# Graph attention on one core: the last half of the mask loaded, signed and packed as two quarters, and the last pair's first row decoded and gathered by itself

## The chip, the cores and the metric

The kernel runs on one core of one Trainium2 chip. The metric is the device time of one execution in microseconds (us). The kernel before takes 815.76 us, the median of three runs from 815.68 to 815.86.

## The reference

The input `x` has 8192 rows of 128 floats, `adj` is a mask of 8192 x 8192 int32 whose entries are 1 with a probability of 0.000488281, so that a row has about four neighbours, and `attn` holds two vectors of 128. The layer is graph attention on a normalised `x`, with `x` added at the end:

```python
h = jnp.maximum(_layernorm(x, axis=-1), 0.0)
s_i = h @ attn[:d]
s_j = h @ attn[d:]
e = jax.nn.leaky_relu(s_i + s_j.T, negative_slope=0.2)
e = e + jnp.where(adj > 0, jnp.float32(0.0), neg_inf)      # neg_inf = -1e9
alpha = jax.nn.softmax(e, axis=1)
x = x + alpha @ h
```

Nearly all of the input is the mask: 268 MB. A row without a neighbour has a softmax over all 8192 nodes, so it needs every row of `h`.

## The kernel before

**Tiles, halves, pairs.** The 8192 rows are cut into 64 tiles of 128 rows, one row to a partition, and two tiles make a pair (32 pairs, `PAIRS`; p = 0 to 31). The row of a pair's first tile is called the first row below, that of the second tile the second row. The mask of a tile comes in two halves of 4096 columns (`HALF`, 2 MB), so there are 128 halves. SP's queue loads them (`load_pair`, `L414`) into a ring of five (`adj_ring`); the load of half n waits until half n - 5 has been signed.

**From the mask to candidates.** ACT signs each half (`sign_tile`, `L614`): one instruction turns the int32 into small floats in `sign_ring` (four halves) and accumulates the row's count into `degree`. TensorE packs the signs of the columns into 1024 words a row, in PSUM (`pack_tile`): two matmuls place a constant (`L1358`), then four matmuls a half add the digits (`L1367`). When a half is signed, its four matmuls are let go, by the semaphore `signed`. DVE takes the eight largest of every quarter of the words (`max_tile`, four MAX8 at `L770`), which gives 32 candidates a row (`cand`).

**From candidates to neighbours.** `find_pair` (`L777` to `L825`) decodes the candidates of both rows together: it unpacks each word into eight codes (`L787`, an AND with a mask of bits, into `terms`), takes the largest eight codes of each row (MAX8 at `L794`, `L795`), joins the two lists and turns the codes into row numbers, `near_id`. A pair has 12 slots (`SLOTS`): four of the first row (`OWN`), four that serve both rows, four of the second. POOL gathers slot by slot 128 rows of `h` from a table in DRAM, one indirect DMA a slot (`gather_pair`, `L521`), into a ring of three pairs (`near`). `flag_pair` (`L834` to `L856`) compares what was found with `degree` and flags the rows with more neighbours than that.

**From neighbours to the output.** `score_pair` (`L907` to `L923`, DVE) adds up the scores of the 16 edges of a pair, `exp_pair` (`L631`, ACT) exponentiates them, `weigh_pair` (`L966` to `L970`, DVE) makes weights of them. For most pairs DVE adds up the weighted rows too, two turns later. The last three pairs (29, 30, 31; `BODY` is 29) are mixed on TensorE: ACT writes each of the 16 weight columns as a diagonal matrix (`write_diagonals`, `L644`), TensorE multiplies the gathered rows by them (`mix_pair`, `L1403` and `L1407`; the profile counts two matmuls for each product in float32), and ACT copies the sums out (`close_pair`, `L649`).

**Other rows.** Flagged rows are listed by a matmul with a one-hot matrix (`key_pair` on DVE, `L862` and `L866`; `L1393` on TensorE) and worked on 128 at a time, with 16 gathers for each such list (`find_deep`, `L979` to `L1012`, and `L532` on POOL). Rows without a neighbour, called lone, are collected for the pairs from 25 on by `lone_mark` (`L1064` to `L1074`), `lone_compact` (`L1083` to `L1106`), `lone_spreads` on TensorE (`L1424`, `L1427`), `lone_bounds` (`L1113` to `L1129`) and `lone_part` (up to `L1147`), exponentiated by ACT (`L670`) and summed over all 8192 rows by 64 steps of TensorE (`lone_matmuls`, `L1443`). A loop for rows that fit nowhere (the far loop) stands at the end and runs one step here.

**Order.** Each engine works through its own stream in the order in which the code lists it, and semaphores tie the streams together; nothing reorders them. The order is written out by hand. In the last turn, p = 31, DVE's stream reads: `max_tile(62)`, `key_pair(30)`, `score_pair(29)`, `max_tile(63)`, `find_pair(31)`, `flag_pair(31)`, `lone_mark`, `key_pair(31)`, `weigh_pair(29)`, `lone_compact`, `score_pair(30)`, `find_deep`, `weigh_pair(30)`, `mark_severe`, `lone_bounds`, `size_loop`, `lone_part`, `score_pair(31)`, `weigh_pair(31)`, the far loop. ACT's stream after the last signing: the diagonals of pair 29, `exp_pair(30)`, `close_pair(29)`, diagonals of pair 30, closing and storing it, the exponentials of the lone rows, then the same for pair 31. TensorE has the products of pair 29 ahead of `lone_spreads`, and those of pairs 30 and 31 behind it.

## Time and profile before

| What | Value |
| --- | --- |
| Median of the timed runs | 815.76 us (815.68 to 815.86) |
| Profiled execution | 813.88 us, of which the span that the profile shows is 812.1 us |
| PE (TensorE matmul) | busy 368.9 us, 45% of the span |
| DVE (VectorE) | busy 615.4 us, 76% |
| ACT (ScalarE) | busy 534.3 us, 66% |
| POOL (GpSimd) | busy 504.5 us, 62% |
| Chain that ended last | DMA 74%, issue 14%, POOL 5%, ACT 3%, DVE 3%, PE 1% |

The profile is of one execution, whose 813.88 us is 1.88 us below the median of the timed runs. Busy shares are means over the whole span. The profile also shows the span in 40 equal slices of 20.3 us: the DMA engines are at 0.9 or more from the 2nd to the 36th slice and move some 390 to 430 GB/s, and in the last four slices it is 132, 33, 56 and 8 GB/s. In these four DVE is at 0.8, 0.9, 0.3 and 0.3, TensorE at 0.6, 0.6, 0.4 and 0.7, POOL at 0.5, 0.5, 0.7 and 0.3. The chain is read from the last instruction back to what released each step; "issue" is time in which the profile shows nothing that the engine waited for.

### The profile page before, as it was taken

Reading aid. Unit: us, or ns where it says so; the run is one execution under the profiler, and the core shown is the slowest. Engines: PE = TensorE matmul, PEld = TensorE weight load, DVE = VectorE, ACT = ScalarE, POOL = GpSimd, SP = SyncE. Lnnn points to the kernel's source line nnn. Section 1 sums busy time; section 2 is a strip of 40 time slices with the busy share of each in tenths; the row PEclk is TensorE's granted clock in tenths of the full one; section 3 lists DMA queues with packets and bytes.
Section 4 is the critical chain, followed back from the end, with each engine's and each line's share of the span. In section 5 each row is a group of like instructions: output and inputs, shape, how many; then the busy total and the mean of one; then the engine's idle time right before and its main releaser. Section 6 shows DMA issues by size and latency. Waiting matters only on the chain.

```text
span 812.1 us, 6394 instructions
## 1 busy us (share of the span) xinstructions
PE 368.9 (45%) x1359; PEld 168.9 (21%) x1378; DVE 615.4 (76%) x2028; ACT 534.3 (66%) x410; POOL 504.5 (62%) x526
## 2 busy tenths in 40 slices
PE   1455334444433344444444344443444545646647
PEld 1222011111111111111111011111111213424636
DVE  6898288677758667797769666797769799898933
ACT  4985676676676767676675767667666677767430
POOL 6720777755556767755547677556547667765573
PEclk9875565555555555555555565555555556877679
DMA  8999999999999999999999999999999999993120
GB/s 344 406 408 429 393 406 408 405 414 411 410 391 412 411 408 406 405 406 407 410 403 406 409 407 408 407 412 413 411 412 408 409 407 411 406 410 132 33 56 8
DMA packets 39719, 301.59 MB, mean 371 GB/s; under 512 B 10682, under 2 KB 17149, under 8 KB 22272
## 3 DMA queue, kind: packets, MB, share of 16 engines
q1 hardware_dynamic: 24032, 277.04, 83.9%
q0 software_dynamic: 15360, 23.88, 8.6%
q10 hardware_dynamic: 288, 0.26, 0.1%
q8 instruction: 11, 0.18, 0.1%
q14 instruction: 28, 0.23, 0.1%
HBM read 303.76 MB, written 8.98 MB: 385 GB/s over the span
## 4 chain that ended last, share of the span: by engine, by line
DMA 74%; issue 14%; POOL 5%; ACT 3%; DVE 3%; PE 1%; POOLq 0%; SPq 0%; DVEq 0%
DMA adj_ring<-in_adj_dram 73%; POOL near L521 3%; ACT sign_ring L614 2%; POOL near_m L532 2%; DMA x_all<-in_x_dram 1%; DVE one_hot L725 1%; ACT h_all L626 1%; PE words L1367 0%; DMA out_dram<-adj_ring 0%; POOL out_dram L562 0%; DVE sums L955 0%; DVE cand L770 0%; POOLq L597 0%; DVE terms L950 0%; POOL adj_ring L553 0%
## 5 line engine op out<-in xcount | busy, mean ns | idle before, releaser
L614 ACT ACTIVATE sign_ring<-adj_ring,half_neg 128x4096 fp8e3<-128x4096 int32 x128 | 474.9, 3710 | 215.3 <-DMA adj_ring<-in_adj_dram 215.3
L521 POOL DMA_INDIRECT near<-h_table,near_id x384 | 391.1, 1019 | 234.2 <-issue 122.8
L1367 PE MATMUL words<-sign_ring,pack_w 128*128 128x512 bf16 x511 | 220.2, 581 | 357.9 <-ACT sign_ring L614 357.6
L770 DVE MAX8 cand<-words 128x8 f32<-128x256 f32 x256 | 90.8, 416 | 113.3 <-PE words L1367 113.3
L1367 PEld LDWEIGHTS words<-sign_ring,pack_w 128*128 128x128 bf16 x512 | 53.9, 125 | 520.7 <-ACT sign_ring L614 453.1
L955 DVE TENSOR_REDUCE sums<-terms 128x128 f32<-128x1024 f32 x58 | 112.2, 1935 | 2.0
L532 POOL DMA_INDIRECT near_m<-h_table,id_m x64 | 65.1, 1017 | 19.5 <-issue 19.5
L950 DVE TENSOR_TENSOR terms<-near,weight 128x512 f32<-128x512 f32 (+1 forms) x87 | 73.4, 871 | 0.0
L1358 PE MATMUL words<-place,place_w 128*128 128x512 bf16 x110 | 55.2, 587 | 7.1 <-DVE key L862 3.7
L1393 PEld LDWEIGHTS listing<-cand,one_hot 128*128 128x128 f32 x128 | 33.0, 316 | 10.6 <-issue 7.3
L1348 PE MATMUL listing<-h_all 128*1 128x128 f32 x128 | 18.6, 316 | 24.8 <-ACT h_all L626 24.8
L1393 PE MATMUL listing<-cand,one_hot 128*128 128x34 f32 x128 | 27.6, 358 | 0.2 <-DVE one_hot L866 0.2
L614 ACT ACTIVATION_READ_ACCUMULATOR sign_ring<-adj_ring,half_neg 128x1 f32 x128 | 23.8, 186 | 0.0
L1443 PE MATMUL rank<-h_all,x_all 128*64 128x129 f32 x128 | 21.0, 343 | 4.6 <-DVE key L862 4.6
L787 DVE TENSOR_TENSOR terms<-cand_i,code_mask 128x512 int32<-128x512 int32 x32 | 22.1, 692 | 1.1
L958 DVE SCALAR_TENSOR_TENSOR x_all<-sums,inv,x_all 128x128 f32<-128x128 f32 x58 | 20.4, 351 | 2.1
L756 DVE TENSOR_TENSOR near<-h_all,terms 128x2048 f32<-128x2048 f32 x8 | 21.4, 2681 | 0.0
L644 ACT ACTIVATE adj_ring<-ident,adj_ring 128x128 f32<-128x128 f32 x48 | 14.3, 387 | 10.7 <-DVE adj_ring L970 10.7
L1443 PEld LDWEIGHTS rank<-h_all,x_all 128*64 128x64 f32 x128 | 20.3, 181 | 4.9 <-DVE key L862 4.9
L626 ACT ACTIVATE h_all<-x_all,terms 128x128 f32<-128x128 f32 x48 | 18.8, 480 | 2.3 <-DVE terms L742 2.3
L498 POOL TENSOR_SCALAR h_all<-x_all,terms 128x128 f32<-128x128 f32 x16 | 13.0, 828 | 11.7 <-DVE terms L742 11.7
L907 DVE TENSOR_SCALAR score<-near,h_all 128x8 f32<-128x8 f32 x32 | 7.0, 220 | 17.1 <-DMA near<-h_table,near_id 17.1
(271 smaller groups left out, 521.7 us busy)
## 6 DMA issues: line engine op xcount, KB each, us to landing
adj_ring<-in_adj_dram SPq DMA_DIRECT2D x128, 2048.0 KB, 24.6
near<-h_table,near_id POOLq DMA_INDIRECT x384, 6.4
h_table<-h_all POOLq DMA_DIRECT2D x4, 1056.0 KB, 14.8
x_all<-in_x_dram SPq DMA_DIRECT2D x4, 1024.0 KB, 9.7
out_dram<-x_all SPq DMA_DIRECT2D x30, 128.0 KB, 24.2
near_m<-h_table,id_m POOLq DMA_INDIRECT x64
out_dram<-x_all ACTq DMA_DIRECT2D x2, 128.0 KB, 3.1
adj_ring<-h_table SPq DMA_DIRECT2D x1, 132.0 KB, 2.6
```

Of the source, the lines that this page charges most:

```text
L521: pool.indirect_dma_start(out=near[:, p % RING, k, :], out_offset=None, in_=table, in_offset=bass.IndirectOffsetOnAxis(ap=near_id[:, p % I ...
L532: pool.indirect_dma_start(out=near_m[:, k, :], out_offset=None, in_=table, in_offset=bass.IndirectOffsetOnAxis(ap=id_m[:, k:k + 1], axis=0 ...
L614: nc.scalar.activation(bytes_of, adj_ring[:, n % HALVES, :].rearrange("p (d r i) -> p d r i", r=2, i=WORDS), ACT.Sign, bias=half_neg[:, :] ...
L626: nc.scalar.activation(h_all[:, t, 0:D], x_all[:, t, :], ACT.Relu, bias=shift[:, t:t + 1], scale=rstd[:, t:t + 1]).then_inc(h_ready, 1)
L770: last = nc.vector.max(out=cand[:, p % 2, t % 2, 8 * q:8 * q + 8], in_=words[t % 3][:, q * PART:(q + 1) * PART])
L787: nc.vector.tensor_tensor(codes[:, :, :, :].rearrange("p a w c -> p (a w) c"), cand_i[:, :, :].rearrange("p a w -> p (a w)").unsqueeze(2). ...
L950: nc.vector.tensor_tensor(terms[:, at, :], near[:, e, slots, 0:D], weight[:, g % 2, weights].unsqueeze(2).broadcast_to([P, at.stop - at.st ...
L955: nc.vector.tensor_reduce(sums[:, a, :], terms[:, :, :].rearrange("p k d -> p d k"), AX.X, ALU.add).then_inc(mixing, 1)
L1358: nc.tensor.matmul(at[:, k * BANK:(k + 1) * BANK], place_w[:, :], place[:, k * BANK:(k + 1) * BANK], start=True, stop=False)
L1367: last = nc.tensor.matmul(at[:, k * BANK:(k + 1) * BANK], pack_w[:, d, :], twins[:, o + k * BANK:o + (k + 1) * BANK], start=False, stop=(d ...
L1393: last = nc.tensor.matmul(listing[:, 0:REC], one_hot[:, p % 2, a, :], cand[:, p % 2, a, :], start=(p % SEG == 0 and a == 0), stop=(p % SEG ...
L1443: last = nc.tensor.matmul(lone_sum[b], part[:, k * e:(k + 1) * e], h_all[:, c * lt + k, 0:ONE + 1], start=(first and k == 0), stop=(final ...
```

## The change

**The last half in two quarters.** Half 127 is loaded by two transfers of 2048 columns, of which the second has a semaphore of its own (`adj_last_in`). ACT signs it by two instructions (`sign_last`); the count of the second goes to `degree_end`. TensorE packs it in two steps of two matmuls, the second released by the second signing. `flag_pair` of the last pair first adds `degree_end` to `degree`.

**The last pair's first row alone.** `find_first_row` decodes the 32 candidates of the first row of pair 31 and writes the four numbers of the slots that only the first row uses. It stands between `max_tile(62)` and `max_tile(63)`. `find_pair(31)` decodes the second row alone and writes the other eight numbers. POOL's first four gathers of pair 31 wait for the first four numbers, the other eight for the rest.

**Two moves in DVE's order.** `score_pair(29)` stood ahead of `max_tile(63)` and now stands behind `flag_pair(31)`. `weigh_pair(29)` stood ahead of `lone_compact` and now stands behind it.

The core of the diff:

```diff
@@ load_pair (SP)
+                    if n < 2 * TILES - 1:
...
+                    else:
+                        sp.dma_start(adj_ring[:, n % HALVES, 0:HALF // 2], adj_t[n // 2, :, HALF:HALF + HALF // 2]) \
+                            .then_inc(adj_in[n % HALVES], 16)
+                        sp.dma_start(adj_ring[:, n % HALVES, HALF // 2:HALF], adj_t[n // 2, :, HALF + HALF // 2:N]) \
+                            .then_inc(adj_last_in, 16)
@@ gather_pair (POOL)
-                pool.wait_ge(near_id_ready, p + 1)
+                if p < PAIRS - 1:
+                    pool.wait_ge(near_id_ready, p + 1)
+                else:
+                    pool.wait_ge(first_id_ready, 1)
...
                 for k in range(SLOTS):
+                    if p == PAIRS - 1 and k == OWN:
+                        pool.wait_ge(near_id_ready, p + 1)
@@ (ACT)
+            def sign_last():
+                n = 2 * TILES - 1
+                for q in range(2):
+                    act.wait_ge((adj_in[n % HALVES], adj_last_in)[q], (16 * (n // HALVES) + 16, 16)[q])
+                    act.wait_ge(packed, n - 3)
+                    at = slice(q * HALF // 2, (q + 1) * HALF // 2)
+                    nc.scalar.activation(sign_ring[:, n % 4, at].rearrange("p (i r) -> p r i", r=2),
+                                         adj_ring[:, n % HALVES, at].rearrange("p (r i) -> p r i", r=2),
+                                         ACT.Sign, bias=half_neg[:, :], saturate=False,
+                                         accum_out=(degree[:, TILES - 1, 1:2], degree_end[:, :])[q]).then_inc(signed, 1)
...
-                sign_tile(2 * p + 1, (1,))
+                if p < PAIRS - 1:
+                    sign_tile(2 * p + 1, (1,))
+            sign_last()
+            act.wait_ge(signed, 4 * PAIRS + 1)
             exp_step(PAIRS - 1)
-            act.wait_ge(signed, 4 * PAIRS)
@@ (DVE)
+            def find_first_row(p):
+                e = p % 2
+                own = slice(0, OWN)
+                dve.wait_ge(maxed, 2 * p + 1)
+                nc.vector.tensor_scalar(cand_i[:, 0, :], cand[:, e, 0, 0:CAND], 1.0 / UNIT, 3.0 * EACH,
+                                        ALU.mult, ALU.add).then_inc(finding_first, 1)
...
+                nc.vector.max(out=best_f[:, 0:8], in_=codes[:, 0, :, :].rearrange("p w c -> p (w c)")) \
+                    .then_inc(finding_first, 1)
...
+                nc.vector.tensor_tensor(near_id[:, p % IDS, own], offset[:, own], unused[:, own], ALU.add) \
+                    .then_inc(first_id_ready, 1)
@@ find_pair (DVE)
+                rows, at = (slice(0, 2), slice(0, SLOTS)) if p < PAIRS - 1 else (slice(1, 2), slice(OWN, SLOTS))
...
-                nc.vector.max(out=best_f[:, 0:8], in_=codes[:, 0, :, :].rearrange("p w c -> p (w c)"))
+                if p < PAIRS - 1:
+                    nc.vector.max(out=best_f[:, 0:8], in_=codes[:, 0, :, :].rearrange("p w c -> p (w c)"))
@@ flag_pair (DVE)
+                if p == PAIRS - 1:
+                    nc.vector.tensor_tensor(degree[:, TILES - 1, 1:2], degree[:, TILES - 1, 1:2], degree_end[:, :],
+                                            ALU.add).then_inc(finding_first, 1)
+                    dve.wait_ge(finding_first, 10)
@@ the turn of a pair (DVE)
-                for g in mixes:
-                    score_pair(g)
+                if p < PAIRS - 1:
+                    for g in mixes:
+                        score_pair(g)
+                else:
+                    find_first_row(p)
...
                 if p == PAIRS - 1:
+                    score_pair(BODY)
                     lone_mark(LAST)
                     key_pair(p)
+                    lone_compact(LAST)
                     weigh_pair(BODY)
-                    lone_compact(LAST)
                     score_pair(BODY + 1)
@@ pack_tile (TensorE)
                     if d % (DIGITS // 2) == 0:
                         pe.wait_ge(signed, n + 1)
+                    elif n == 2 * TILES - 1:
+                        pe.wait_ge(signed, n + 2)
```

In the code of the changed kernel the lines have other numbers: `max_tile` is `L798` there, `find_first_row` `L809` to `L837`, `find_pair` `L846` to `L892`, `score_pair` `L978` to `L994`, `weigh_pair` `L1037` to `L1041`, `lone_compact` `L1154` to `L1177`, the gathers `L536`.

DVE's stream in the last turn, from the end of `key_pair(30)` (`L866`) to the last MAX8 of the mask (`L770`), before; `L907` to `L923` are the scoring of pair 29, and `near_in2` counts its gathers:

```order
L866 TENSOR_SCALAR one_hot<-entry,key 128x128
L907 TENSOR_SCALAR score<-near,h_all 128x8 [waits near_in2]
L909 TENSOR_SCALAR score<-near,h_all 128x4
L911 TENSOR_SCALAR score<-near,h_all 128x4
L914 SCALAR_TENSOR_TENSOR valid_score<-invalid,score 128x16 [waits scoring]
L917 SCALAR_TENSOR_TENSOR leaky<-valid_score 128x16 [waits scoring]
L921 TENSOR_REDUCE top<-leaky 128x2 [waits scoring]
L923 TENSOR_TENSOR below<-leaky,top 128x16 [waits scoring]
L770 MAX cand<-words 128x8 [waits packed]
L770 MAX cand<-words 128x8 x3
L781 TENSOR_SCALAR cand_i<-cand 128x64 [waits maxed]
```

The same place after, where `one_hot` is again the end of `key_pair(30)` and `L809` to `L837` are `find_first_row`:

```order
L937 TENSOR_SCALAR one_hot<-entry,key 128x128
L809 TENSOR_SCALAR cand_i<-cand 128x32 [waits maxed]
L812 TENSOR_SCALAR cand_i<-cand_i 128x32 [waits finding_first]
L815 TENSOR_TENSOR terms<-cand_i,code_mask 128x256 [waits finding_first]
L820 MAX best<-terms 128x8 [waits finding_first]
L823 TENSOR_SCALAR power<-best 128x4 [waits finding_first]
L825 SCALAR_TENSOR_TENSOR unused<-best,fill 128x4
L828 TENSOR_SCALAR chunk<-power 128x4 [waits finding_first]
L831 SCALAR_TENSOR_TENSOR unused<-unused,best 128x4 [waits finding_first]
L834 SCALAR_TENSOR_TENSOR offset<-chunk,power 128x4 [waits finding_first]
L837 TENSOR_TENSOR near_id<-offset,unused 128x4 [waits finding_first]
L798 MAX cand<-words 128x8 [waits packed]
```

The seven steps of the scoring have left the place, and ten steps of the first row's decoding stand in it; the MAX8 row waits for the same semaphore as before.

DVE's stream further on in the last turn, before: the end of `lone_mark` is just ahead, `L862` and `L866` are `key_pair(31)`, `L966` to `L970` are `weigh_pair(29)`, and `L1083` to `L1092` the beginning of `lone_compact`:

```order
L862 SCALAR_TENSOR_TENSOR key<-flag,rank 128x2 [waits ranked]
L866 TENSOR_SCALAR one_hot<-entry,key 128x128 [waits keyed]
L866 TENSOR_SCALAR one_hot<-entry,key 128x128
L966 TENSOR_REDUCE total<-weight 128x2 [waits weight_ready]
L968 RECIPROCAL inv<-total 128x2 [waits mixing]
L970 TENSOR_TENSOR adj_ring<-weight,inv 128x16 [waits mixing]
L1083 TENSOR_TENSOR adj_ring<-h_all,adj_ring 128x56
L1086 TENSOR_TENSOR adj_ring<-adj_ring,h_all 128x56 [waits lone1]
L1089 TENSOR_REDUCE adj_ring<-adj_ring 128x4 [waits lone1]
```

After, first from the end of `flag_pair(31)` (`L924` and `L927`, which count the flags) to the beginning of `lone_mark` (`L1135`):

```order
L927 TENSOR_TENSOR prior<-prior,flag 128x1 [waits flagging]
L978 TENSOR_SCALAR score<-near,h_all 128x8 [waits near_in2]
L980 TENSOR_SCALAR score<-near,h_all 128x4
L982 TENSOR_SCALAR score<-near,h_all 128x4
L985 SCALAR_TENSOR_TENSOR valid_score<-invalid,score 128x16 [waits scoring]
L988 SCALAR_TENSOR_TENSOR leaky<-valid_score 128x16 [waits scoring]
L992 TENSOR_REDUCE top<-leaky 128x2 [waits scoring]
L994 TENSOR_TENSOR below<-leaky,top 128x16 [waits scoring]
L1135 MEMSET adj_ring 128x128 [waits bounds_ready,flags_ready]
```

and then from the end of `lone_compact` (`L1169` to `L1177`) to the first step of `score_pair(30)` (`L978`):

```order
L1169 TENSOR_REDUCE adj_ring<-rank 128x1
L1171 SCALAR_TENSOR_TENSOR adj_ring<-rank,adj_ring 128x1 [waits lone1]
L1174 TENSOR_SCALAR adj_ring<-adj_ring 128x1 [waits lone1]
L1177 TENSOR_SCALAR x_all<-adj_ring 128x14 [waits lone1]
L1037 TENSOR_REDUCE total<-weight 128x2 [waits weight_ready]
L1039 RECIPROCAL inv<-total 128x2 [waits mixing]
L1041 TENSOR_TENSOR adj_ring<-weight,inv 128x16 [waits mixing]
L978 TENSOR_SCALAR score<-near,h_all 128x8 [waits near_in0]
```

The scoring of pair 29 now stands between `flag_pair(31)` and `lone_mark`, and its weighing has moved from ahead of `lone_compact` to behind it.

POOL's stream at the gathers of the last two pairs, 30 and 31, before; `L532` are the gathers of the last list:

```order
L521 DMA near<-h_table,near_id 128x132 [waits pair_mixed,near_id_ready]
L521 DMA near<-h_table,near_id 128x132 x11
L521 DMA near<-h_table,near_id 128x132 [waits pair_mixed,near_id_ready]
L521 DMA near<-h_table,near_id 128x132 x11
L532 DMA near_m<-h_table,id_m 128x132 [waits mixed_m_ready,id_m_ready]
```

and after, where the gathers are `L536` and `L547`:

```order
L536 DMA near<-h_table,near_id 128x132 [waits pair_mixed,near_id_ready]
L536 DMA near<-h_table,near_id 128x132 x11
L536 DMA near<-h_table,near_id 128x132 [waits pair_mixed,first_id_ready]
L536 DMA near<-h_table,near_id 128x132 x3
L536 DMA near<-h_table,near_id 128x132 [waits near_id_ready]
L536 DMA near<-h_table,near_id 128x132 x7
L547 DMA near_m<-h_table,id_m 128x132 [waits mixed_m_ready,id_m_ready]
```

The twelve gathers of pair 31 are now four and eight, each group with a wait of its own; nothing else on POOL has moved.

## Rows read from the trace of the kernel before

**Rows 1.** Chain of waits: start us, duration us, engine and line

```profile
750.94 4.96 issue
```

**Rows 2.** Timeline of POOL: start us, us, instruction, [idle before <-releaser]

```profile
756.11 1.00 POOL L521 DMA_INDIRECT near<-h_table,near_id  x1 [5.17 <-DVE near_id L822]
...
770.44 1.81 POOL L521 DMA_INDIRECT near<-h_table,near_id  x1 [0.31 <-issue]
```

**Rows 3.** Timeline of ACT, 739 to 785 us, same columns

```profile
740.45 3.71 ACT L614 ACTIVATE sign_ring<-adj_ring,half_neg 128x4096 fp8e3<-128x4096 int32 x1 [1.23 <-DMA adj_ring<-in_adj_dram]
...
745.89 3.71 ACT L614 ACTIVATE sign_ring<-adj_ring,half_neg 128x4096 fp8e3<-128x4096 int32 x1 [1.63 <-DMA adj_ring<-in_adj_dram]
749.50 0.19 ACT L614 ACTIVATION_READ_ACCUMULATOR sign_ring<-adj_ring,half_neg 128x1 f32 x1
...
759.59 4.78 ACT L644 ACTIVATE adj_ring<-ident,adj_ring 128x128 f32<-128x128 f32 x16 [9.79 <-DVE adj_ring L970]
764.27 0.20 ACT L631 ACTIVATE weight<-below 128x16 f32<-128x16 f32 x1
...
774.00 1.06 ACT L670 ACTIVATE adj_ring<-adj_ring 128x1024 f32<-128x1024 f32 x1 [1.27 <-DVE adj_ring L1147]
...
776.10 4.78 ACT L644 ACTIVATE adj_ring<-ident,adj_ring 128x128 f32<-128x128 f32 x16 [0.65 <-DVE adj_ring L970]
```

**Rows 4.** Timeline of PE, 744 to 786 us, same columns

```profile
745.10 1.91 PE L1367 MATMUL words<-sign_ring,pack_w 128*128 128x512 bf16 x4
749.75 1.23 PE L1367 MATMUL words<-sign_ring,pack_w 128*128 128x512 bf16 x4 [2.73 <-ACT sign_ring L614]
...
760.50 3.62 PE L1407 MATMUL words<-near,adj_ring 128*128 128x128 f32 x16
...
764.24 1.95 PE L1407 MATMUL words<-near,adj_ring 128*128 128x128 f32 x16
...
766.91 0.35 PE L1427 MATMUL words<-adj_ring 128*16 128x1 f32 x8
...
773.82 0.49 PE L1403 MATMUL words<-x_all,ident 128*128 128x128 f32 x2 [1.51 <-DMA near<-h_table,near_id]
...
780.01 2.51 PE L1407 MATMUL words<-near,adj_ring 128*128 128x128 f32 x16
```

**Rows 5.** Timeline of DVE, 744 to 786 us, same columns

```profile
751.01 1.43 DVE L770 MAX8 cand<-words 128x8 f32<-128x256 f32 x4 [3.05 <-PE words L1367]
...
752.93 0.69 DVE L787 TENSOR_TENSOR terms<-cand_i,code_mask 128x512 int32<-128x512 int32 x1
...
759.41 0.24 DVE L1083 TENSOR_TENSOR adj_ring<-h_all,adj_ring 128x56 f32<-128x56 f32 x1
...
761.60 0.23 DVE L907 TENSOR_SCALAR score<-near,h_all 128x8 f32<-128x8 f32 x1
...
762.95 0.17 DVE L923 TENSOR_TENSOR below<-leaky,top 128x16 f32<-128x16 f32 x1
...
763.46 0.41 DVE L986 TENSOR_TENSOR terms<-cand_m,code_mask 128x256 int32<-128x256 int32 x1
...
766.23 0.16 DVE L966 TENSOR_REDUCE total<-weight 128x2 f32<-128x16 f32 x1
...
768.12 0.17 DVE L1113 COPY adj_ring<-words 128x16 f32<-128x16 f32 x1
...
773.88 0.22 DVE L907 TENSOR_SCALAR score<-near,h_all 128x8 f32<-128x8 f32 x1
...
775.03 0.17 DVE L923 TENSOR_TENSOR below<-leaky,top 128x16 f32<-128x16 f32 x1
```

**Rows 6.** Windows: stretch, length; PE PEld DVE ACT POOL busy (xcount); PEclk; DMA; GB/s

```profile
762.00:764.00 2.00, 2.00 (x11) 2.00 (x11) 1.79 (x11) 2.00 (x9) 1.39 (x3) 0.50 0.10 14
764.00:766.00 2.00, 2.00 (x19) 2.00 (x19) 1.83 (x9) 0.47 (x3) 1.70 (x2) 0.97 0.13 21
778.00:780.00 2.00, 2.00 (x10) 2.00 (x11) 0.93 (x5) 2.00 (x8) 1.69 (x2) 0.50 0.53 138
```

More of the change, by code:

```diff
@@ L158, in graph_attention_kernel @@
         degree = sb("degree", [P, TILES, 2], fp32)
+        degree_end = sb("degree_end", [P, 1], fp32)
         fullest = sb("fullest", [P, 2], fp32)
@@ L293, in graph_attention_kernel @@
         adj_in = [sem(f"adj_in{i}") for i in range(HALVES)]
+        adj_last_in = sem("adj_last_in")
         consts = sem("consts")
@@ L318, in graph_attention_kernel @@
         near_id_ready = sem("near_id_ready")
+        finding_first = sem("finding_first")
+        first_id_ready = sem("first_id_ready")
         flagging = sem("flagging")
@@ L779, in find_pair @@
                 e = p % 2
+                rows, at = (slice(0, 2), slice(0, SLOTS)) if p < PAIRS - 1 else (slice(1, 2), slice(OWN, SLOTS))
+                n = rows.stop - rows.start
                 dve.wait_ge(maxed, 2 * p + 2)
-                nc.vector.tensor_scalar(cand_i[:, :, :], cand[:, e, :, 0:CAND], 1.0 / UNIT, 3.0 * EACH,
+                nc.vector.tensor_scalar(cand_i[:, rows, :], cand[:, e, rows, 0:CAND], 1.0 / UNIT, 3.0 * EACH,
                                         ALU.mult, ALU.add).then_inc(find, 1)
@@ L784, in find_pair @@
                 dve.wait_ge(find, f + 1)
-                nc.vector.tensor_scalar(cand_i[:, :, :], cand_i[:, :, :], EACH, None, ALU.bitwise_xor).then_inc(find, 1)
+                nc.vector.tensor_scalar(cand_i[:, rows, :], cand_i[:, rows, :], EACH, None, ALU.bitwise_xor) \
+                    .then_inc(find, 1)
                 dve.wait_ge(find, f + 3)
                 nc.vector.tensor_tensor(
-                    codes[:, :, :, :].rearrange("p a w c -> p (a w) c"),
-                    cand_i[:, :, :].rearrange("p a w -> p (a w)").unsqueeze(2).broadcast_to([P, 2 * CAND, CHUNKS]),
-                    code_mask[:, :].unsqueeze(1).broadcast_to([P, 2 * CAND, CHUNKS]), ALU.bitwise_and) \
+                    codes[:, rows, :, :].rearrange("p a w c -> p (a w) c"),
+                    cand_i[:, rows, :].rearrange("p a w -> p (a w)").unsqueeze(2).broadcast_to([P, n * CAND, CHUNKS]),
+                    code_mask[:, :].unsqueeze(1).broadcast_to([P, n * CAND, CHUNKS]), ALU.bitwise_and) \
                     .then_inc(find, 1)
@@ L832, in flag_pair @@
                     dve.wait_ge(flags_ready, p)
-                dve.wait_ge(signed, 4 * p + 4)
+                dve.wait_ge(signed, 4 * p + (4 if p < PAIRS - 1 else 5))
+                if p == PAIRS - 1:
+                    nc.vector.tensor_tensor(degree[:, TILES - 1, 1:2], degree[:, TILES - 1, 1:2], degree_end[:, :],
+                                            ALU.add).then_inc(finding_first, 1)
+                    dve.wait_ge(finding_first, 10)
                 nc.vector.scalar_tensor_tensor(lacking[:, :], missing[:, :], 2.0, degree[:, ts, 0],
```

40 lines of the change are left out of this document (32 added, 8 removed).

## The prediction

> **What bounds the kernel now.** I read the chain of waits first. Most of it is the loading of `adj`, which the change leaves alone up to its last half. Then the chain runs along POOL: the gathers of pair 30, an idle stretch of 4.96 us, the twelve gathers of pair 31 and what follows them [rows 1]. The timeline of POOL says what the idle stretch was: the first gather of pair 31 waits 5.17 us for `near_id`, which DVE writes; the twelve gathers then start 14.33 / 11 = 1.30 us apart [rows 2]. That idle stretch is what the change fills. The chain, however, names only the releaser that came last, so I looked next at who else arrives where the gathers are used. The last of them lets TensorE's `L1403` go at 773.82 [rows 4]; DVE begins the scoring of the same pair (`L907`) at 773.88, with no idle time before it [rows 5]. So two chains arrive within 0.06 us: the gathers, and a row of DVE work that has been dense since 751.01, where the row shows its last wait, for TensorE [rows 5]. Shortening one of them alone gives nothing. The question is what the change does to DVE's.
>
> Behind that point there is one chain: scoring, ACT's diagonals of pair 31 (776.10), TensorE's products of that pair, the far loop and `lone_matmuls` [rows 3, 4]. A shift of the scoring passes through to the end.
>
> **Signing and packing in quarters.** A half of 4096 elements takes ACT 3.71 us and 1024 elements take 1.06 us (`L670`), so an element costs 2.65 / 3072 = 0.863 ns and a quarter of 2048 takes 1.94 us [rows 3]. The half before ends at 740.45 + 3.71 = 744.16. The last two halves were waited for until 740.45 and 745.89, 5.44 us apart, so in the order of the queue the first quarter is due near 743.2 and the second near 745.9. ACT then runs from 744.16 to 746.10 and to 748.04, and the read-out ends 0.09 later, at 748.13, where it was 749.69: **1.56 us earlier**. The cover is 1.0 us for the first quarter but only 0.2 us for the second. What two transfers cost instead of one no row shows. An earlier landing gains nothing, because ACT is the limit then; for a later one the nearest row is the 5.44 us, and a quarter of it, 1.4 us, is my bound. I take 0, since halves have been landing one behind the other at the rate of the queue.
>
> The Trainium skill, "DMA: Bandwidth & Descriptors", section "Anatomy of one DMA — SWDGE (gpsimd) path", gives each transfer of that path a fixed 2.0 us beside its bytes. Paid in full behind the first quarter it would let the second land near 747.9, and the end would come 1.8 us later than by my sum. The two waits 5.44 us apart for 2 MB, with others queued behind, show no such step.
>
> Four matmuls took 1.23 us there and 1.91 us one half earlier [rows 4]; two take half of either, 0.62 to 0.96, say 0.80. Before, DVE started 1.32 us after the read-out's end, 0.09 of it outside the matmuls. So the last MAX8 row starts at 748.13 + 0.09 + 0.80 = 749.02 instead of 751.01: **1.99 us earlier** (1.83 to 2.17). DVE must be free by then. It was idle for 3.05 us before 751.01, behind the scoring of pair 29. A scoring costs 1.24 us (773.88 to 775.03, and half of the last step's 0.17 until the next starts); it leaves this place at about 746.7, and the decoding of the first row comes in. The whole decoding of a pair runs from 752.44, the end of the MAX8 row, to POOL's release at 756.11: 3.67 us. One row needs neither the second MAX8 (1.43 / 4 = 0.36) nor half of the AND (`L787`, 0.69, against 0.41 for 256 elements in `L986`: 0.28) nor four small steps of 0.2 us each. That leaves 2.2 us: POOL could be released at 748.9, and DVE is free a little before [rows 2, 5].
>
> **The gathers.** POOL's last gather of pair 30 ended at 750.94, and the next can start 0.30 later, at 751.24 [rows 1, 2]. The first row's numbers are there 2.3 us before that. Four gathers reach to 756.45, and the second row's numbers come at about 753.5. So POOL never waits: **4.87 us earlier** (756.11 - 751.24), and the last gather lands near 768.95.
>
> **DVE's chain.** The second row's decoding is shorter by a MAX8 and half the AND: 0.64. Together with 1.99 that is 2.63 us earlier. Against it stand the sum of the two degrees with its wait, 0.20, and the scoring of pair 29, 1.24, which used to fill idle time and now stands in the dense part. POOL now gathers while DVE decodes, and before it was idle there; beside gathers the scoring of pair 30 reached its last step 1.35 us after its first (761.60 to 762.95), that of pair 31 after 1.15, so I allow 0 to 0.5 and take 0.1. At `lone_mark` DVE is therefore **1.1 us earlier**, not 4.87.
>
> **ACT behind it.** `weigh_pair` of pair 29 now comes after `lone_compact`, which takes 761.60 - 759.41 = 2.19 us [rows 5]. So the diagonals of pair 29 start 2.19 - 1.1 = 1.1 us *later*, at 760.68 [rows 3]. Sixteen of them take 4.78, and `exp_pair(30)`, queued behind them on ACT, moves from 764.27 to 765.36, done at 765.56. DVE would weigh pair 30 at 766.23 - 1.1 = 765.13 and must now wait until 765.60: it is **0.63 us** ahead.
>
> **TensorE behind that.** The products of pair 29 wait for those diagonals: their start moves from 760.50 to about 761.1. A slot takes 3.62 / 8 = 0.45 us in the first row's products and 1.95 / 8 = 0.24 in the second's [rows 4]; the granted clock was 0.50 up to about 764 and 1.0 behind it, 1.2 and 2.4 GHz [rows 6]. If it rises at the same time, 1.3 slots fewer are done by then, and the end moves from 766.19 by 0.3; if it rises later with the work, by 0.8. I take 0.55. `lone_spreads` stands behind them on TensorE and ended at 767.26, now 767.81. DVE reads its result at 768.12 - 0.63 = 767.49 and waits until 767.86: DVE is **0.26 us** ahead. From there `lone_part` runs as before, and the scoring of pair 31 starts at 773.62, long after its gathers. ACT's own queue (diagonals of pair 30 to about 772.0, closing, store) is done by about 773.2 and so not later.
>
> **Sum.** 0.3 us off. The profiled execution is 813.88 us (a span of 812.1 and 1.78 around it), so 813.6 for it; the median of the timed runs is 815.76, so **815.5**. With the bounds above this case reaches from 1.1 us off to 0.5 us on: 814.7 to 816.3. About 0.2%, 1.6 us, is what a measurement of this kernel can tell from no change, so this counts as the same.
>
> **Rivals.** *The gathers alone bound the end.* Then all 4.87 us come through: 810.9. For it speaks the chain, which names POOL; against it DVE's 773.88 without idle time. Chance 0.04.
>
> *TensorE stays at the low clock through the products of pair 29* (slower). It now pauses between its identity products and the first diagonal, where it used to run on. With 16 slots of 0.45 and the second row's identity product the products end at 761.07 + 7.24 + 0.5 = 768.8, `lone_spreads`, which ended 1.07 us behind them at the high clock, at 769.9 to 770.9, and DVE is 1.8 to 2.9 us behind, say 2.3: 818.1. It decides against the change as soon as the products end after 767.05. For it speaks that the clock rose only 3.5 us after the products had begun; against it that from 761.1 on the work is as dense as before [rows 4, 6]. Chance 0.12. The Trainium skill, "TensorE: Matmul & The Clock Gate", "Part 1: The HAM clock gate", says that throttled is the default, that activity releases it and that the moment varies from run to run of one kernel. The two levels in rows 6 agree; that the moment varies no row here shows.
>
> *The clock stays high in the last products.* Pair 31's ran at 0.50 from 778 on [rows 6]; they ended at 780.01 + 2.51 = 782.52, while the last diagonal was written at 776.10 + 4.78 = 780.88. At the high clock they would end near 781.2, 1.3 us sooner: with the 0.3 that is 814.2. For it speaks that the diagonals start a little sooner after TensorE's work on pair 30; against it that the pair's identity products, which stood in between at 773.82, now go early too. Chance 0.13, half of it beyond 1.6 us.
>
> *The second quarter lands late* (slower). Its cover is 0.2 us. At the bound it lands at 747.3, signing ends 1.2 us later than reckoned, and the end is 0.9 us on: 816.7. It turns the gain into a loss from 0.5 us of lateness on. Chance 0.06. This is what the page on DMA would do here; its figure would give 817.3.
>
> **How the numbers follow.** The forecast has 0.65. Faster by over 0.2%: 0.04, half of 0.13, and 0.03 for the low end of the forecast, 0.14. Slower: most of 0.12, with a part of 0.06 and some for what I overlook on ACT and DVE, 0.14. The same: 0.72. The range runs from 813.9, below the third rival, to 817.9, just short of the second one's full price, and leaves out the first.
>
> **What would show it.** Right: POOL goes from pair 30 to pair 31 without a gap, its last gather near 765.6; the last MAX8 row at about 749.0; diagonals of pair 29 at about 760.7, *later* than before; a wait of DVE for ACT before it weighs pair 30, and one for TensorE before `lone_bounds`; the scoring of pair 31 within half a microsecond of 773.9 although its gathers landed near 769. Wrong: DVE idle before the scoring of pair 31, or that scoring 3 us earlier (the gathers did bound it); or the signing of the last quarter ending after 749.

## The result, and the profile after

The changed kernel takes 817.74 us (median of 20 runs, 815.92 to 819.29) against 815.72 for the kernel before in the same series (one of its 20 runs took 1247.77, the others 814.13 to 817.21): a ratio of 1.0024 with a 95% interval of 1.0016 to 1.0031, so 1.3 to 2.5 us **slower**. The forecast was 815.5, 0.3 us faster. The time lies inside the range of 813.9 to 817.9, but the forecast has the wrong sign and is 2.3 us off (+2.0 against -0.3).

The profiled execution of the changed kernel took 817.65 us (a span of 815.9). That is 3.8 us more than that of before, but the two executions were apart already before the change begins: half 119, eight halves ahead of the end, is signed from 700.86 on before and from 702.62 on after. The kernels are the same up to there, so this 1.76 us is chance of the loading (over all traces of this case that point lies between 700.50 and 703.24), and all that follows is counted from half 119. ACT's timeline, of before and of after (start us, us, instruction, what the idle time before it waited for):

```profile
700.86 3.71 ACT L614 ACTIVATE sign_ring<-adj_ring,half_neg 128x4096 fp8e3<-128x4096 int32 x1 [1.77 <-DMA adj_ring<-in_adj_dram]
```

```profile
702.62 3.71 ACT L629 ACTIVATE sign_ring<-adj_ring,half_neg 128x4096 fp8e3<-128x4096 int32 x1 [1.76 <-DMA adj_ring<-in_adj_dram]
...
738.75 3.71 ACT L629 ACTIVATE sign_ring<-adj_ring,half_neg 128x4096 fp8e3<-128x4096 int32 x1 [2.80 <-DMA adj_ring<-in_adj_dram]
...
743.99 3.71 ACT L629 ACTIVATE sign_ring<-adj_ring,half_neg 128x4096 fp8e3<-128x4096 int32 x1 [1.44 <-DMA adj_ring<-in_adj_dram]
...
747.70 1.99 ACT L639 ACTIVATE sign_ring<-adj_ring,half_neg 128x2048 fp8e3<-128x2048 int32 x1
...
749.68 1.99 ACT L639 ACTIVATE sign_ring<-adj_ring,half_neg 128x2048 fp8e3<-128x2048 int32 x1
...
764.26 4.78 ACT L670 ACTIVATE adj_ring<-ident,adj_ring 128x128 f32<-128x128 f32 x16 [3.95 <-DVE adj_ring L1041]
...
779.46 4.79 ACT L670 ACTIVATE adj_ring<-ident,adj_ring 128x128 f32<-128x128 f32 x16 [0.64 <-DVE adj_ring L1041]
```

The first row after is half 119, then come halves 125 and 126, the two quarters, and the diagonals of pairs 29 and 31. The quarters do what they were meant to: 1.99 us each, the second directly behind the first. But half 125 already starts 36.13 us behind half 119, where it was 34.56 before, and half 126 at 41.37 instead of 39.59 ([rows 3] has 740.45). The whole difference, point by point (the last packet's end is from the trace's packet records):

| us after the signing of half 119 | before | after | difference |
| --- | --- | --- | --- |
| last packet of the mask ends | 44.45 | 46.25 | +1.80 |
| last MAX8 row starts | 50.15 | 50.27 | +0.12 |
| scoring of pair 31 starts | 73.02 | 74.63 | +1.61 |
| end of the span | 111.29 | 113.30 | +2.01 |

So the loading gives 1.80 back of what quarters win, 1.49 us are lost between the MAX8 row and the last scoring, and 0.40 behind it. These are two executions, one of each kernel, and the traces of the runs below show how far each step can be trusted. From the MAX8 row to the scoring, the seven kernels with the old order (before, e1, e2, e5, e6, e9, e10) take 22.87 to 23.15 us, the two with the new one 24.37 (after) and 24.86 (e3): this loss is clear. From the scoring to the end, the eleven kernels with the same order there (all but e8, e11 and e12) take 37.70 to 39.10 (before 38.27, after 38.67): the 0.40 is inside that spread. The MAX8 row starts 50.15 to 51.02 us after half 119 in the seven kernels with one transfer and 49.93 to 50.88 in the four that sign in quarters: before is the earliest of its seven, so that the +0.12 is no more than "about the same". The rows of DVE and POOL that answer to [rows 5] and [rows 2]:

```profile
752.89 1.42 DVE L798 MAX8 cand<-words 128x8 f32<-128x256 f32 x4 [1.96 <-PE words L1444]
...
769.18 0.17 DVE L1037 TENSOR_REDUCE total<-weight 128x2 f32<-128x16 f32 x1 [0.47 <-ACT weight L657]
...
771.73 0.17 DVE L1184 COPY adj_ring<-words 128x16 f32<-128x16 f32 x1 [0.52 <-PE words L1504]
...
777.25 0.22 DVE L978 TENSOR_SCALAR score<-near,h_all 128x8 f32<-128x8 f32 x1
```

```profile
753.27 1.00 POOL L536 DMA_INDIRECT near<-h_table,near_id  x1 [0.30 <-issue]
...
767.60 1.00 POOL L536 DMA_INDIRECT near<-h_table,near_id  x1 [0.30 <-issue]
```

DVE waits for `exp_pair(30)` (0.47) and for `lone_spreads` (0.52), as forecast, and reaches the scoring of pair 31 with no idle time before it. POOL no longer stops ahead of the first gather of pair 31 (753.27): its last gather starts 64.98 us after half 119, 4.6 earlier than before (69.58). The chain of waits shows who set the end. POOL, 5% before, is gone from it; PE has 4% where it had 1%. This is the page's line on it, after:

```profile
DMA 76%; issue 11%; PE 4%; DVE 4%; ACT 4%; POOL 0%; DVEq 0%; ACTq 0%
```

### The profile page after: what moved, and what is told of

It reads as the page before. It is cut to its first block, busy times and chain, and to the rows that moved or that the text cites. A ratio compares the mean times of both kernels' runs of the same rounds, so it can differ in the third digit from the quotient of the medians.

```text
span 815.9 us, 6408 instructions
## 1 busy us (share of the span) xinstructions
PE 373.0 (46%) x1359; PEld 170.9 (21%) x1378; DVE 616.8 (76%) x2038; ACT 534.5 (66%) x412; POOL 504.3 (62%) x526
## 4 chain that ended last, share of the span: by engine, by line
DMA 76%; issue 11%; PE 4%; DVE 4%; ACT 4%; POOL 0%; DVEq 0%; ACTq 0%
DMA adj_ring<-in_adj_dram 76%; ACT sign_ring L629 2%; PE words L1520 2%; PE words L1484 1%; DVE one_hot L753 1%; ACT h_all L652 1%; DMA x_all<-in_x_dram 1%; ACT sign_ring L639 0%; DVE cand L798 0%; DVE adj_ring L1210 0%; DVE adj_ring L1214 0%; DVE adj_ring L1218 0%; PE words L1594 0%; PE words L1444 0%; POOL out_dram L577 0%
## 5 line engine op out<-in xcount | busy, mean ns | idle before, releaser
L536 POOL DMA_INDIRECT near<-h_table,near_id x384 | 390.3, 1016 | 231.2 <-issue 123.2
L798 DVE MAX8 cand<-words 128x8 f32<-128x256 f32 x256 | 90.9, 417 | 115.0 <-PE words L1444 115.0
L547 POOL DMA_INDIRECT near_m<-h_table,id_m x64 | 65.0, 1016 | 19.6 <-issue 18.9
L853 DVE TENSOR_TENSOR terms<-cand_i,code_mask 128x512 int32<-128x512 int32 (+1 forms) x32 | 21.9, 684 | 1.1
L978 DVE TENSOR_SCALAR score<-near,h_all 128x8 f32<-128x8 f32 x32 | 6.8, 213 | 16.7 <-DMA near<-h_table,near_id 16.7
L1484 PE MATMUL words<-near,adj_ring 128*128 128x128 f32 x96 | 16.5, 342 | 4.9 <-ACT adj_ring L670 4.9
```

The costliest lines, as they stand in the source:

```text
L536: pool.indirect_dma_start(out=near[:, p % RING, k, :], out_offset=None, in_=table, in_offset=bass.IndirectOffsetOnAxis(ap=near_id[:, p % I ...
L547: pool.indirect_dma_start(out=near_m[:, k, :], out_offset=None, in_=table, in_offset=bass.IndirectOffsetOnAxis(ap=id_m[:, k:k + 1], axis=0 ...
L798: last = nc.vector.max(out=cand[:, p % 2, t % 2, 8 * q:8 * q + 8], in_=words[t % 3][:, q * PART:(q + 1) * PART])
L1484: last = nc.tensor.matmul(at, diagonal[:, i % 2, a * own + k, :], near[:, g % RING, slot, 0:D], start=False, stop=(k == own - 1))
```

## Why the last half lands late: experiments on the loading

**e1: two transfers, nothing else.** ACT waits for both and signs the whole half.

```diff
-    sp.dma_start(adj_ring[:, n % HALVES, :], adj_t[n // 2, :, HALF:N]).then_inc(adj_in[n % HALVES], 16)
+    for q in range(2):
+        at = slice(q * HALF // 2, (q + 1) * HALF // 2)
+        sp.dma_start(adj_ring[:, n % HALVES, at], adj_t[n // 2, :, HALF:N][:, at]).then_inc(adj_in[n % HALVES], 16)
```

> The kernel before, with the last half loaded by two transfers of 2048 columns; ACT waits for both and signs the half at once, nothing else is changed. In the two profiles the last half was complete 1.8 us later after the change than before, counted from the signing of half 119 (46.8 us against 45.0). Theory A, the two transfers make it late: this kernel is 1.8 us slower than before (817.5). Theory B, the loss of 2.0 us arises behind the last MAX8 row and the late landing was chance of one execution: no difference (within 0.5 us of 815.7).

818.08 us, a ratio of 1.0028 (1.0016 to 1.0041): 2.3 us slower. Two transfers instead of one cost what was lost, with no other edit. Theory A stands.

**e2: loading, signing and packing in quarters**, with decoding, gathers and order as before.

> Loading, signing and packing in quarters alone, with the decoding, the gathers and the order of DVE as before. The last MAX8 row and the numbers for POOL then come earlier together, so both chains that meet at the last scoring move. Theory A (two transfers land 1.8 us late): 2.0 us won by signing and packing less 1.8, so -0.2 us, within 0.5 us of before. Theory B (the loss is behind the MAX8 row): -2.0 us, 813.7.

815.62 us, 0.9996 (0.9987 to 1.0005). What the quarters win, the loading takes back. Theory A again; theory B's 813.7 is outside.

**e5, e6: smaller packets, or more transfers?** e5 keeps one transfer and cuts each row into two pieces (the order keeps them apart); e6 makes two transfers of 64 rows each, with whole rows.

```diff
+    sp.dma_start(adj_ring[:, n % HALVES, :].rearrange("p (q i) -> p q i", q=2)[:, ::-1, :],
+                 adj_t[n // 2, :, HALF:N].rearrange("p (q i) -> p q i", q=2)[:, ::-1, :]).then_inc(...)   # e5
...
+    at = slice(q * P // 2, (q + 1) * P // 2)
+    sp.dma_start(adj_ring[at, n % HALVES, :], adj_t[n // 2, at, HALF:N]).then_inc(...)                   # e6, q = 0, 1
```

> The kernel before, with the last half still loaded by one transfer, but in two pieces of 8 KB a row (the second piece of a row ahead of the first, so that they cannot be joined to 16 KB). Two transfers of 8 KB pieces cost 2.3 us (e1). Theory P, the size of the packets is what costs: this kernel is 2 us slower than before, too (817.8), and its trace shows packets of 8 KB that take up to 1 us instead of 0.31 some 30 us after the signing of half 119. Theory T, the number of transfers is what costs: no difference (815.7).

> The kernel before, with the last half loaded by two transfers of 64 rows each, in packets of 16 KB as before; ACT waits for both. Theory P (size of packets): no difference (815.7). Theory T (number of transfers): 2 us slower, 817.8.

e5: 815.82 us, 0.9999 (0.9990 to 1.0007): small packets cost nothing. e6: 825.7 us, 1.0114 (1.0100 to 1.0129): 9.7 us slower, five times what theory T said. That two transfers of whole rows cost far more than two of half rows fits neither theory, so the number alone is not it.

**e9, e10: which bytes the engines read at a time.** The rows of a tile lie 64 rows of 32 KB, 2 MB, apart. In e1 the DMA engines read the same 8 KB of such rows until they are through with the first quarter. e9 also makes two transfers, but each takes two pieces of 4 KB of every row, one from the first 2048 columns of the half and one from the second; e10 is one transfer in pieces of the same size.

```diff
+    to = adj_ring[:, n % HALVES, :].rearrange("p (b q i) -> p b q i", b=2, q=2)
+    of = adj_t[n // 2, :, HALF:N].rearrange("p (b q i) -> p b q i", b=2, q=2)
+    for q in range(2):
+        sp.dma_start(to[:, :, q, :], of[:, :, q, :]).then_inc(adj_in[n % HALVES], 16)                    # e9
```

> The kernel before, with the last half loaded by two transfers whose columns interleave: each takes two pieces of 4 KB of every row, from both ends of the half. One transfer in pieces of 8 KB cost nothing (e5), two transfers of one quarter of 8 KB each cost 2.3 us (e1). Theory N, two transfers behind one another are what slows the packets: 2 us slower than before (818). Theory W, that all engines read the same 8 KB of rows 2 MB apart is what slows them: within 0.7 us of before.

> The control for e9: one transfer of the last half in pieces of 4 KB, each row from its end to its beginning. Both theories: no difference from before (815.9), as with pieces of 8 KB. If it is 2 us slower, small pieces cost by themselves and e9 tells nothing.

e9: 816.72 us, 1.0008 (0.9998 to 1.0019); e10: 816.28 us, 1.0007 (0.9996 to 1.0019). By the times alone e9 is 0.5 us over before, between the theories and nearer to W; its interval reaches to 1.5 us, short of N's 2. The packet records are clearer, though they are of one execution each, e9's of its fastest (814.91). The longest packet is that of the packets that end from 28 to 36 us after half 119, the usual one their median:

| kernel | last half | last packet, us after half 119 | longest packet, us (usual) |
| --- | --- | --- | --- |
| before | one transfer, 16 KB | 44.45 | 0.69 (0.62) |
| e5 | one transfer, pieces of 8 KB | 44.57 | 0.39 (0.31) |
| e10 | one transfer, pieces of 4 KB | 44.70 | 0.21 (0.16) |
| e9 | two transfers, interleaved columns, 4 KB | 44.72 | 0.73 (0.16) |
| e1 | two transfers, one quarter each, 8 KB | 46.41 | 1.41 (0.32) |
| after | the same | 46.25 | 1.22 (0.32) |
| e6 | two transfers, 64 rows each, 16 KB | 55.60 | 1.89 (1.54) |

The lateness is in every kernel with two transfers by quarters: the last packet ends at 46.64 in e2, 46.58 in e4 and 45.82 in e12, and at 44.49 to 44.54 in the four others with one transfer (e3, e7, e8, e11).

The packets of 16 KB that were still under way beside the quarters stall as well (up to 1.94 us in e1, 1.56 after), which is why half 125 is late, although it stands ahead of the quarters. The landings show whose packets these are. Every half is counted in by 16 steps of its semaphore, and of half 127 before, fifteen are there by 36.86 us after half 119, the sixteenth only at 45.00; from 37 us on there is one packet of the mask under way at a time. So one sixteenth of each of the last halves runs some 8 us behind the rest, and it alone decides when the half is complete. Its landings are these:

| last step of the semaphore, us after half 119 | before | e9 | e1 | after |
| --- | --- | --- | --- | --- |
| half 124 | 29.31 | 29.38 | 29.45 | 29.41 |
| half 125 | 34.53 | 34.78 | 36.47 | 36.11 |
| half 126 | 39.57 | 39.64 | 41.72 | 41.35 |
| half 127 (its first transfer) | 45.00 | 45.22 (42.52) | 46.88 (44.25) | 46.90 (44.27) |

After, 1.58 of the 1.90 us arise in this last part of half 125, which is loaded while the other fifteen are at the quarters; once it is loaded alone it is nearly as fast as before (5.24 and 5.55 us for the last two halves, 5.04 and 5.43 before). What puts it 8 us behind no run here shows. The slower packets show in the windows from 28 to 32 us after half 119: before, e5, e9, e1, after and e6 in this order. The columns are the stretch and its length, the busy times of PE, PEld, DVE, ACT and POOL, PEclk, the DMA engines' busy share and GB/s:

```profile
728.90:732.90 4.00, 2.46 (x12) 1.81 (x11) 3.50 (x14) 2.70 (x1) 1.02 (x1) 0.50 1.01 411
```

```profile
730.10:734.10 4.00, 2.46 (x11) 1.79 (x10) 3.57 (x15) 2.63 (x1) 1.02 (x1) 0.50 1.01 403
```

```profile
729.90:733.90 4.00, 2.46 (x11) 1.79 (x10) 3.51 (x14) 2.63 (x1) 1.03 (x1) 0.50 0.97 359
```

```profile
731.20:735.20 4.00, 2.46 (x11) 1.66 (x10) 3.45 (x15) 2.48 (x1) 1.02 (x1) 0.50 1.02 302
```

```profile
730.60:734.60 4.00, 2.46 (x11) 1.55 (x10) 2.87 (x13) 2.55 (x1) 1.02 (x1) 0.50 0.96 279
```

```profile
729.90:733.90 4.00, 2.46 (x12) 1.81 (x11) 3.52 (x14) 0.00 (x0) 1.02 (x1) 0.50 1.09 176
```

The DMA engines are equally busy in all six, 0.96 to 1.09, and move 411 and 403 GB/s with one transfer, 359 with two interleaved ones, 302 and 279 with two by quarters, 176 with two by rows. So the transfers by quarters do not wait; their packets run slower. That reading one narrow band of columns of all rows is the reason is what e9 against e1 supports; it is not shown, since e6 reads all the columns of its rows and is slower still. The Trainium skill, "DMA: Bandwidth & Descriptors", section "Latency and other measured facts", says that copies of rows whose pitch is a large power of two run slower, and offers, as an inference, that streams in step then meet in the same part of the memory. Whether that is at work here is open: the pitch is 2 MB in every run, which that page of the Trainium skill lists as slow for copies between tensors in HBM, and whole halves are loaded here at 411 GB/s. Whether the packets meet where they are read or where they are written no run here separates, and why e6 is so slow stays open.

## Where the rest went: experiments on the order

**e3: the first row and the two moves, without the quarters. e7: the first row with the two moves undone. e4: the changed kernel with the moves undone.**

```diff
                 else:
                     find_first_row(p)
+                    score_pair(BODY)
...
-                    score_pair(BODY)
                     lone_mark(LAST)
                     key_pair(p)
-                    lone_compact(LAST)
                     weigh_pair(BODY)
+                    lone_compact(LAST)
```

> The first row alone, its four gathers and the two moves in DVE's order, with the last half loaded, signed and packed whole. The MAX8 row should then start where it did before, and from there the last scoring of the changed kernel stood 1.5 us later than before in the profiles, the end 1.9. Theory A: +1.7 us, 817.4. Theory B: the whole loss of 2.0 and the 2.0 that the quarters no longer win, +4.0 us, 819.7.

> The first row decoded and gathered by itself, without the quarters, and with the two moves undone (the scoring of pair 29 behind the decoding of the first row, the weighing of pair 29 ahead of the compaction). By the steps of the prediction DVE is 0.64 us ahead of before from the second row's decoding on, less 0.2 for slower steps beside gathers: 0.4 us faster than before, 815.3. By the runs so far, if effects add up: e3 (817.39) less what undoing the moves gave (817.74 - 814.43 = 3.31) is 814.1.

> The changed kernel with the two moves in DVE's order undone: the scoring of pair 29 behind the decoding of the first row, ahead of the last MAX8 row, and the weighing of pair 29 ahead of the compaction of lone rows. The changed kernel's profile shows DVE idle for 1.96 us ahead of that row, which is room for a scoring of 1.24. Against the changed kernel the diagonals of pair 29 start 1.24 + 2.15 us sooner, so DVE has no waits for ACT and TensorE (0.47 and 0.52) and reaches the last scoring 2.2 us sooner. Theory A: 815.5, 0.2 us under before. Theory B, where the waits and the clock behind the MAX8 row carry the loss: 813.5 or less.

e3: 817.39 us, 1.0026 (1.0017 to 1.0036). e7: 815.79 us, 0.9998 (0.9989 to 1.0007). e4: 814.43 us, 0.9982 (0.9973 to 0.9991). e3 is where its theory A had it; e4 lies halfway between its two theories. The moves cost 1.6 us without the quarters (e3 against e7 in the medians, 2.3 by the ratios) and 3.3 with them (817.74 against 814.43); the two were only undone together, so that the share of each is not known. In e3's trace both waits of DVE are there; in e4's and e7's neither is. DVE in e3, the weighing of pair 30 and the beginning of `lone_bounds`:

```profile
767.18 0.17 DVE L1014 TENSOR_REDUCE total<-weight 128x2 f32<-128x16 f32 x1 [0.41 <-ACT weight L640]
...
769.98 0.17 DVE L1161 COPY adj_ring<-words 128x16 f32<-128x16 f32 x1 [0.72 <-PE words L1479]
```

e7 gained less than either reckoning (0.2 us, inside its noise, against 0.4 and 1.7), e4 more (1.3 against 0.2). By the trace the MAX8 row starts 50.82 us after half 119 in e4 and 50.30 in e7, so the quarters should not favour e4, and the traces end 111.05 us (e4) and 110.88 (e7) after half 119, with e4's of its slowest execution and e7's of its fastest. This difference, between two kernels whose intervals just overlap (0.9989 to 0.9991), is not settled.

**e11, e8, e12: letting the early gathers count.** DVE scores and weighs pair 31 ahead of `lone_part`, and ACT writes its diagonals behind those of pair 30. e11 does that alone, e8 on top of e7, e12 on top of e4.

```diff
-                    for c in range(LONE_PARTS[LAST]):
-                        lone_part(LAST, c)
                     break
...
             score_pair(BODY + 2)
             weigh_pair(BODY + 2)
+            for c in range(LONE_PARTS[LAST]):
+                lone_part(LAST, c)
...
             write_diagonals(BODY + 1)
+            exp_pair(BODY + 2)
+            write_diagonals(BODY + 2)
             close_pair(BODY + 1)
             store_pair(BODY + 1)
             for c in range(LONE_PARTS[LAST]):
                 exp_lone(LAST, c)
-            exp_pair(BODY + 2)
-            write_diagonals(BODY + 2)
             close_pair(BODY + 2)
```

> The kernel before with only the last order of e8: pair 31 scored and weighed ahead of lone_part, its diagonals right behind those of pair 30, and no early gathers. If gathers and DVE arrive together before (773.82 and 773.88), DVE now waits at the scoring from 770.2 until 773.8 for the gathers, and the diagonals start at about 775.9, where they started at 776.1: no gain, 815.7 (within 0.6 us of before). If the order alone is what e8 won, 812.1 to 812.5.

> The kernel of e7, and behind it the order that lets the early gathers count: DVE scores and weighs pair 31 ahead of lone_part (3.73 us), ACT writes the diagonals of pair 31 right behind those of pair 30, and closes and stores pair 30 and exponentiates the lone rows after them. The gathers of pair 31 should have landed near 769 by the clock of the profile before, the diagonals of pair 30 end near 771.2, so those of pair 31 start near 772.3 where they started at 776.1. If the chain scoring, diagonals, products, far loop sets the end, 3.4 us faster than e7's steps give, 812 to 812.5; if the order of these steps is not what bounds the end (the lone rows' sums or POOL's gathers do), no faster than e7.

> The kernel of e8 with the quarters of the changed kernel. Two transfers make the last half 1.9 us late and signing and packing in quarters win 2.0 us back: no difference from e8, 812 (within 0.8 us).

e11: 815.67 us, 0.9993 (0.9982 to 1.0004): nothing gained, as expected. e8: 812.05 us, 0.9956 (0.9941 to 0.9970), 3.9 us off in the medians and 3.6 by the ratio. e12: 810.9 us (5 runs), 0.9946 (0.9933 to 0.9959), the lowest of all; it is 1.2 us under e8 in the medians, 0.8 by the ratios, whose intervals overlap, so a gain from the quarters is not shown. The scoring of pair 31 in e11 and in e8 (DVE), then the diagonals of pair 31 in both (ACT):

```profile
775.20 0.23 DVE L907 TENSOR_SCALAR score<-near,h_all 128x8 f32<-128x8 f32 x1 [2.71 <-DMA near<-h_table,near_id]
```

```profile
772.00 0.24 DVE L955 TENSOR_SCALAR score<-near,h_all 128x8 f32<-128x8 f32 x1
```

```profile
777.42 4.78 ACT L644 ACTIVATE adj_ring<-ident,adj_ring 128x128 f32<-128x128 f32 x16 [0.65 <-DVE adj_ring L970]
```

```profile
774.46 4.79 ACT L653 ACTIVATE adj_ring<-ident,adj_ring 128x128 f32<-128x128 f32 x16 [0.65 <-DVE adj_ring L1018]
```

In e11 DVE is there 2.71 us early and waits for the gathers. In e8 the gathers have landed and it does not wait; counted from half 119 (702.40 and 702.35) the diagonals start 2.9 us sooner. Either chain shortened alone, e7 or e11, gives nothing; both give 3.6 to 3.9 us.

## Why the prediction was wrong

**The step that failed** is the one on the loading: "What two transfers cost instead of one no row shows. ... I take 0, since halves have been landing one behind the other at the rate of the queue." It cost 1.80 us in the trace and 2.3 in e1, more than the bound of 1.4 that I had given it. The sign that the text named for it, a signing of the last quarter that ends after 749, was there: 751.67, or 749.91 without the 1.76 of chance ahead of half 119. The rows of before could not show it, since all transfers of the mask there read whole halves; a bound from the time between two landings holds for a transfer that comes later in its turn, not for packets that slow each other and those ahead of them. The rival "the second quarter lands late" names the place, but with a chance of 0.06 and 0.9 us of loss it was far too small, and it thought of the second quarter only; halves 125 and 126 were late already. It was not the second quarter that ACT waited for: it landed at 46.90 us after half 119, and ACT was busy with the first until 47.06, because half 126 had come 1.78 late. The Trainium skill's fixed cost of a transfer ("DMA: Bandwidth & Descriptors", "Anatomy of one DMA — SWDGE (gpsimd) path"), which the page states for transfers issued by POOL and not for SP's queue, would have given 817.3, near the result, but not by that mechanism: e9, with two transfers as well, lands 0.02 us behind e10 with one.

**The other steps**, with what they measured after:

- Signing and packing in quarters: 1.99 forecast. The last MAX8 row stands 1.68 closer behind the last packet (1.80 - 0.12). Right, 0.3 short: the last two matmuls took 1.03 us where 0.80 was reckoned.
- DVE from the MAX8 row to `lone_mark`: 0.9 longer forecast (1.54 added, 0.64 saved). `L1066` and `L1137` stand 6.64 and 7.34 behind the row: 0.70. Right.
- The diagonals of pair 29, behind the MAX8 row: 1.1 + 1.99 = 3.09 later forecast, 2.79 measured (11.37 against 8.58). Right, and with it DVE's waits: 0.47 and 0.37 forecast, 0.47 and 0.52 measured.
- The scoring of pair 31, behind the MAX8 row: 1.99 - 0.26 = 1.73 later forecast, 1.49 measured. Right.
- The gathers 4.87 earlier: 4.6 measured, and they gained nothing, as forecast. The rival that lets them bound the end is refuted by e7 (no gain) and by e11 and e8 together.
- Behind the scoring, no change forecast: 0.40 longer, inside the spread of the traces (37.70 to 39.10). The products of pair 31 took 6.79 us (779.92 to 786.71) where it had been 5.96 (776.56 to 782.52), and ran at the low clock for longer, the opposite of the third rival. These are the windows from their beginning on, before (776 to 778 is at 0.94, and 778 to 780 is in [rows 6]) and after; PEclk is the third number from the end:

```profile
780.00:782.00 2.00, 2.00 (x15) 2.00 (x14) 0.15 (x1) 0.89 (x4) 1.39 (x3) 0.71 0.16 30
```

```profile
780.00:782.00 2.00, 2.00 (x10) 2.00 (x10) 0.34 (x3) 2.00 (x8) 1.70 (x2) 0.50 0.52 121
782.00:784.00 2.00, 2.00 (x11) 2.00 (x11) 0.59 (x3) 2.00 (x8) 1.39 (x3) 0.50 0.13 37
784.00:786.00 2.00, 2.00 (x13) 2.00 (x13) 0.00 (x0) 0.25 (x1) 1.70 (x2) 0.59 0.03 2
```

- TensorE at the low clock through the products of pair 29 (the second rival): they took 5.90 us (764.71 to 770.61) where it had been 5.69 [rows 4], and the forecast's price for the low clock throughout was over 7.2. It did not happen.

The sum of the misses is 2.11 for the MAX8 row (from -1.99 to +0.12), less 0.24, and 0.40: 2.27, which is the distance from -0.3 to +2.0. That it closes so well is partly luck: the sum is taken from two traces, and that their ends lie as far apart as the medians is chance, with single traces of kernels that are timed alike (before, e2, e5, e7, e9, e10, e11) ending 110.88 to 113.27 us after half 119. What the runs confirm without the traces is the cost of two transfers (e1), that the quarters win no more than that (e2), and the cost of the new order (e3).

## What to carry to other kernels

Cutting a transfer so that its first part can be used sooner is not free: price it by a run that cuts it and changes nothing else. Of the three cuts tried here, only the one in which each transfer takes pieces of every row from both parts of the half (e9) landed on time; the one by rows (e6) was the worst, and e9's cut was not tried with signing in two steps. Look at what part of a transfer lands last: here one sixteenth decided. Where two chains arrive together, shorten both in one change, or expect nothing; that the idle engine stands in the chain of waits says only that it came last. A step that another engine waits for (here the weighing, for ACT) should not be put behind one that nobody waits for, and a step moved out of idle time into a dense row costs its full length there (the scoring was reckoned at 1.24 us; no run moved one step alone).

## What was not expected of the hardware

Two transfers of one quarter of the columns each slowed each other's packets, and those ahead of them, to several times their usual length: 8 KB in up to 1.41 us instead of 0.32 (e1). With two transfers of 64 rows each the DMA engines moved 176 GB/s, and a packet of 16 KB took 1.54 us in the median instead of 0.62 (e6). One sixteenth of the last half landed some 8 us behind the rest, at 45.00 us where the others were there by 36.86 (before).

The same four matmuls of the last packing took 1.23 us before [rows 4] and 1.89 in e11, with nothing in front of them changed, and the MAX8 row behind them starts 50.15 and 50.91 us after half 119. The windows have the granted clock, before and then e11:

```profile
749.70:751.10 1.40, 1.35 (x7) 0.91 (x7) 0.09 (x1) 0.10 (x1) 1.00 (x1) 0.77 0.17 38
```

```profile
751.30:753.30 2.00, 1.91 (x6) 1.00 (x7) 0.00 (x0) 0.14 (x2) 1.00 (x1) 0.50 0.17 38
```

The clock rose to the high level during the first and stayed at the low one in the second. The Trainium skill, "TensorE: Matmul & The Clock Gate", "Part 1: The HAM clock gate", says that the moment of release varies between runs of one kernel; these two, which are the same up to there, agree. It is worth 0.7 us of the last MAX8 row, about as much as several of the steps above.
